# Giving a quarter of a long convolution's transposes to the DMA engines, with ScalarE and VectorE work re-ordered around it

## The chip, the core and the metric

The kernel runs on one core of a Trainium2 chip. The metric is the device time of one execution in microseconds (us), from the hardware; lower is better. The engines are named as in the profile: PE is TensorE (with PEld, its weight loads), ACT is ScalarE, DVE is VectorE, POOL is GpSimd, SP is SyncE, whose queue (SPq) issues nearly all DMAs here.

## What is computed

There are 64 batches (NB), 128 channels (H) and 2048 time steps (T). First each batch's channels are mixed by one of 16 weight matrices, with a residual. Then each channel is convolved over time with its own long kernel K, masked behind a length, and added.

```python
x = x + einsum('bct,bcd->bdt', x, weights[condition])          # step 1
K = 2 * real(einsum('hn,hnl->hl', Ct, exp(dtA[:, :, None] * arange(2048))))   # per channel, 64 modes
y = irfft(rfft(x, 4096) * rfft(K, 4096))[..., :2048] + x * D[:, None]         # step 2: causal convolution
x = x + y * (arange(2048) < length[:, None])
```

## The kernel before

**Two stages.** In the first some 325 us the mixing matmuls run (`L529`), batch by batch, and their results u go to a scratch tensor in HBM, laid out by channel; beside them VectorE works out tables for K. The rest, some 750 us, is the convolution, done as a state-space scan in blocks: time is cut into 8 blocks of Q = 256, and the work goes by **pairs of channels**, 64 pairs (`PAIRS`), one after the other. The change is in this second stage alone.

**One pair.** `u_row` holds a pair's two channels as rows: 128 partitions (64 batches by 2 halves of time) by 4 groups `g` of 256 values, in f32. The matmuls want time on the partitions, so PE transposes each 128x128 piece into a PSUM bank (`transpose_u`, `L541`): 16 a pair, four (g = 0 to 3) into each of banks 4 to 7; the bank is called q = 0 to 3 (channel q // 2, half-block q % 2). ACT copies a bank as the f16 high part into `u_t` (`u_hi`, step "u" of ACT, `L722`), and DVE writes the f16 remainder beside it (`u_lo`, step "u" of DVE, `L986`). Then

- `inputs_to_state` (`L555`, 12 matmuls) adds up what each block puts into the state. It needs all four quarters of `u_t`, and `gt_sb`, which is made by two DMA transposes of `g_sb` (`L317`);
- `advance` for j = 1 to 6 (`L567`, 6 matmuls each) carries the state from block to block. Each needs the state before it: ACT copies its high part out of PSUM (`state_hi`, "s", `L730`), DVE its low part (`state_lo`, "s", `L991`), and only then may PE go on. I call the states s1 to s7;
- `out_part` for k = 0 to 7 (`L590`, `L596`, `L599`) makes the outputs from `u_t`, from the taps `toep`, and from the states. ACT takes them out of PSUM (`out_evac`, "o", `L738`), DVE lays the unmasked values over them (`overlay`, "o", `L1016`), SP stores them.

**Two helpers of `out_part`.** `toep` holds zeros in part of its lower 64 partitions; `fold_toeplitz` ("t", `L1008`) copies taps there. `first_half` ("x", `L1001`, two copies a pair, of f16 64x2048) builds `x_t` out of `u_t`.

**Slots.** Every engine has the same outer loop: slot c does, interleaved in an order written out by hand (`steps` in each engine's `slot`), the states of pair c, the outputs of pair c - 1, and the transposes of pair c + 1. On PE, slot c is out_part(0), out_part(1), `inputs_to_state(c)`, then out_part(k) and advance(k - 1) for k = 2 to 7; two transposes are put into each out_part, `between(2k)` and `between(2k + 1)`. Engines work through their lists strictly in order, with semaphores between them. So a step of DVE that is late makes all the steps behind it in the list late.

**GpSimd** makes the factors for later pairs, without waiting for the slot: `g_lo` (`L424`, after ACT's `g_hi`, step "g", `L674`), then at once the products of the pair after that: twice g_x (`L415`), twice g_y (`L415`), and g_x minus g_y (`L419`).

**SP's order in a slot:** load half of `u_row`, the two transposes of `g_sb`, two stores, load the other half of `u_row`, load `toep`, two stores (which wait for DVE's overlay).

Of the kernel before, what the change touches and what calls it, by code (L numbers as in the profile page):

```python
# [40 lines left out]
WAVES = 5  # L41
XS = 6
# [24 lines left out]
def build(nc, x, cond, length, w_in, log_dt, c_in, log_a, a_im, d_in, out):  # L67
# [6 lines left out]
    with ctx:  # L74
# [16 lines left out]
        eyes = sb("eyes", [P, 2, NM], F16)  # L91
        swap = sb("swap", [P, 2, NM], F16)
# [103 lines left out]
        s_st, s_sth, s_stl = (sem(n) for n in ("s_st", "s_sth", "s_stl"))  # L196
        s_xt, s_tz = sem("s_xt"), sem("s_tz")
# [56 lines left out]
        def _(sp):  # L254
# [65 lines left out]

            def store_out(i, c, h):
# [25 lines left out]
            def slot(i, c):  # L347
# [129 lines left out]
        def _(pe):  # L477
# [55 lines left out]
            def transpose_u(i, c, k):  # L533

                q, g, n = k // NG, k % NG, UN * i + c
                if k % 8 == 0:
# [6 lines left out]
                if g == NG - 1:  # L543
# [105 lines left out]
        def _(act):  # L649
# [94 lines left out]
            first = (("u", 0, 3), ("g", 2, 0), ("s", 0, 1), ("s", 0, 2), ("s", 0, 3), ("u", 1, 0), ("s", 0, 4),  # L744
                     ("s", 0, 5), ("u", 1, 1), ("s", 0, 6), ("u", 1, 2))

            def slot(i, c):
                steps = (("s", c - 1, 7), ("u", c, 3), ("o", c - 2, 3), ("g", c + 2, 0), ("u", c + 1, 0),
                         ("o", c - 1, 0), ("s", c, 1), ("s", c, 2), ("u", c + 1, 1), ("s", c, 3),
                         ("o", c - 1, 1), ("s", c, 4), ("s", c, 5), ("u", c + 1, 2),  # L750
                         ("s", c, 6), ("o", c - 1, 2))
                for what, of, k in steps if c else first:
# [20 lines left out]
        def _(dve):  # L773
# [295 lines left out]
```

## Time and profile before

| | |
|---|---|
| three runs, median (lowest to highest) | 1081.11 us (1080.15 to 1083.68) |
| profiled execution | 1082.12 us, of which its span is 1080.3 us |
| granted TensorE clock, mean | 0.996 |
| PE, DVE, ACT, POOL busy | 93%, 71%, 51%, 47% of the span |
| mean of one `u_hi` (ACT, 512 columns) and one `state_hi` (128 columns) | 595 and 276 ns |
| mean of one `u_lo` (DVE, 512 columns) and one `state_lo` (128 columns) | 689 and 290 ns |

The busy times are of one profiled execution. A matmul's busy time overlaps that of the next, so PE's work is better read from the starts of its rows in the timeline. Rows of the timeline carry the start, the duration, the engine and the line; what stands in brackets is how long the engine sat idle just before, and what released it. A row's duration on DVE and POOL takes in time that the instruction spends issued but held up.

### The profile page before, as it was taken

The page shows a single profiled execution, that of the slowest core. Times are in us where ns is not written, and L with a number is a line of the kernel's source. Part 1 is how long each engine was busy: PE and PEld are TensorE (multiplying, and loading weights), DVE is VectorE, ACT ScalarE, POOL GpSimd, SP SyncE. Part 2 cuts the span into 40 slices and gives each one's busy share as a digit, 9 for nine tenths or more (in the row PEclk, how much of TensorE's full clock was granted, in tenths as well). Part 3 has the DMA queues.
Part 4 walks back from the last instruction along what each step waited for, and adds up shares of the span by engine and source line. Part 5 has one row for each costly group of instructions (what it writes and reads, how often), then busy time and mean ns, then how long its engine had stood idle before and what let it go on. Part 6 is the DMA issues. An engine that isn't in the chain of part 4 may idle for free.

```text
span 1080.3 us, 29253 instructions
## 1 busy us (share of the span) xinstructions
PE 1004.6 (93%) x11632; PEld 739.8 (68%) x11632; DVE 772.3 (71%) x1711; ACT 548.5 (51%) x1166; POOL 502.7 (47%) x545
## 2 busy tenths in 40 slices
PE   8977788777899999999999999999999999999998
PEld 5322234233347888888888788888888888888886
DVE  4989940000017888888888888888888888888885
ACT  2634334244444556556456555555555555555553
POOL 2200042101205556656666665665665665665530
PEclk9999999999999999999999999999999999999999
DMA  8999999999989999999999999999999999999994
GB/s 343 423 423 423 424 422 422 377 424 424 423 326 294 284 271 262 228 227 224 217 239 233 214 238 224 225 234 228 222 232 226 234 221 229 225 225 232 208 223 118
DMA packets 169543, 304.96 MB, mean 282 GB/s; under 512 B 78194, under 2 KB 111346, under 8 KB 161218
## 3 DMA queue, kind: packets, MB, share of 16 engines
q1 hardware_dynamic: 169090, 302.64, 98.4%
q8 instruction: 94, 1.54, 0.6%
q14 instruction: 39, 0.32, 0.1%
q10 hardware_dynamic: 160, 0.26, 0.1%
q0 software_dynamic: 160, 0.20, 0.1%
HBM read 152.37 MB, written 134.41 MB: 265 GB/s over the span
## 4 chain that ended last, share of the span: by engine, by line
PE 74%; DMA 18%; ACT 3%; DVE 2%; issue 2%; SPq 1%; ACTq 0%
DMA u_scratch<-stage 17%; PE bank L590 16%; PE bank L599 15%; PE bank L555 13%; PE bank L541 10%; PE bank L529 7%; PE bank L567 7%; PE bank L596 5%; ACT stage L708 2%; DVE x_t L1001 1%; PE bank L608 1%; DMA x_f<-in_x 1%; DVE st_sb L991 0%; ACT ring L708 0%; DVE u_t L986 0%
## 5 line engine op out<-in xcount | busy, mean ns | idle before, releaser
L590 PE MATMUL bank<-toep,u_t 128*128 128x192 f16 (+1 forms) x3072 | 342.7, 220 | 2.0 <-issue 1.8
L599 PE MATMUL bank<-g_sb,st_sb 128*128 128x256 f16 x1536 | 305.9, 273 | 0.5 <-issue 0.4
L529 PE MATMUL bank<-x_f,w_buf 128*128 128x512 f32 x512 | 237.3, 608 | 57.2 <-ACT stage L708 35.5
L541 PE MATMUL bank<-ident,u_row 128*128 128x128 f32 x1024 | 277.4, 274 | 0.2
L730 ACT ACTIVATE st_sb<-bank 128x128 f16<-128x128 f32 x448 | 123.8, 276 | 289.6 <-PE bank L567 198.0
L590 PEld LDWEIGHTS bank<-toep,u_t 128*128 128x128 f16 x3072 | 231.3, 98 | 16.3 <-issue 2.4
L529 PEld LDWEIGHTS bank<-x_f,w_buf 128*128 128x128 f32 x512 | 93.4, 192 | 192.4 <-issue 109.8
L1016 DVE COPY_PREDICATED o_sb<-mask,u_row 128x512 f32<-128x512 uint8 x256 | 205.8, 804 | 16.6 <-issue 16.5
L986 DVE SCALAR_TENSOR_TENSOR u_t<-bank,u_t 128x512 f16<-128x512 f32 x256 | 176.2, 689 | 37.4 <-ACT u_t L722 35.4
L596 PE MATMUL bank<-toep,x_t 128*128 128x64 f16 x2048 | 188.3, 193 | 1.9 <-issue 1.9
L431 POOL TENSOR_TENSOR lam_sb<-eyes,lam_v 128x512 f16<-128x512 f16 x64 | 75.2, 1176 | 235.7 <-PE bank L567 235.7
L722 ACT ACTIVATE u_t<-bank 128x512 f16<-128x512 f32 x256 | 152.2, 595 | 54.4 <-PE bank L541 50.7
L708 ACT ACTIVATE stage<-bank 128x1024 f32<-128x1024 f32 x100 | 96.8, 1021 | 148.7 <-DMA u_scratch<-stage 124.1
L991 DVE TENSOR_TENSOR st_sb<-bank,st_sb 128x128 f16<-128x128 f32 x448 | 129.7, 290 | 56.2 <-ACT st_sb L730 52.6
L596 PEld LDWEIGHTS bank<-toep,x_t 128*128 128x128 f16 x2048 | 157.5, 98 | 2.1 <-issue 2.1
L555 PE MATMUL bank<-u_t,gt_sb 128*128 128x448 f16 x768 | 155.7, 352 | 1.3 <-DVE u_t L986 1.3
L738 ACT ACTIVATE o_sb<-bank 128x512 f32<-128x512 f32 x256 | 153.2, 599 | 4.1 <-PE bank L599 4.0
L599 PEld LDWEIGHTS bank<-g_sb,st_sb 128*128 128x128 f16 x1536 | 149.3, 98 | 5.8
L541 PEld LDWEIGHTS bank<-ident,u_row 128*128 128x128 f32 x1024 | 143.8, 141 | 9.7 <-issue 1.5
L567 PE MATMUL bank<-st_sb,lam_sb 128*128 128x64 f16 x2304 | 130.0, 193 | 4.8 <-DVE st_sb L991 3.4
L439 POOL TENSOR_TENSOR w_buf<-w_f,ident 128x128 f32<-128x128 f32 x64 | 33.5, 527 | 210.3 <-PE bank L529 205.1
L567 PEld LDWEIGHTS bank<-st_sb,lam_sb 128*128 128x128 f16 x2304 | 107.4, 97 | 32.9 <-issue 10.0
(135 smaller groups left out, 912.6 us busy)
## 6 DMA issues: line engine op xcount, KB each, us to landing
x_f<-in_x SPq DMA_DIRECT2D x64, 1024.0 KB, 19.6
u_row<-u_scratch SPq DMA_DIRECT2D x128, 512.0 KB, 5.7
out<-o_sb SPq DMA_DIRECT2D x254, 256.0 KB, 3.8
u_scratch<-stage SPq DMA_DIRECT2D x50, 1024.0 KB, 17.8
toep<-k_scratch SPq DMA_DIRECT2D x64, 256.0 KB, 6.0
u_scratch<-ring SPq DMA_DIRECT2D x13, 512.0 KB, 14.7
u_scratch<-kept SPq DMA_DIRECT2D x10, 448.0 KB, 7.0
gt_sb<-g_sb SPq DMA_TRANSPOSE x124, 5.4
```

What stands on the lines that cost most here:

```text
L529: last = pe.matmul(bank[:, 4 * (n % 2) + k, :], w_buf[n % XS][:, :], x_f[n % XS][:, k * 512:(k + 1) * 512], start=True, stop=True)
L541: last = pe.transpose(bank[:, 4 + q, g * P:(g + 1) * P], u_row[c % 4][:, h, g, tb * P:(tb + 1) * P], ident[:, :])
L555: last = pe.matmul(bank[:, h, 0:(NJ - 1) * NB], gt_sb[c % 2][:, h, a, 1 - tb, :], u_t[c % 4][:, h, tb, b, 0:(NJ - 1) * NB], start=(m == 0) ...
L567: last = pe.matmul(bank[:, h, at(j):at(j) + NB], lam_sb[c % 2][:, h, a, :, :].rearrange("p k m -> p (k m)"), st_sb[c % 2][:, h, b, at(j):a ...
L590: pe.matmul(bank[:, y, col + tb * P + NM:col + Q], u[:, h, tb, a, rows_], t[:, h, b, NM:Q - tb * P], start=first, stop=False, skip_group_c ...
L596: pe.matmul(bank[:, y, col + tb * P:col + tb * P + NM], x_t[c % 2][:, h, tb, rows_], t[:, h, b, 0:NM], start=False, stop=False, skip_group ...
L599: last = pe.matmul(bank[:, y, col:col + Q], st[:, h, a, gr * ROWS:(gr + 1) * ROWS], g[:, h, b, :], start=False, stop=(m == 2), skip_group_ ...
L722: act.activation(u_t[c % 4][:, q // 2, q % 2, 0, :], bank[:, 4 + q, :], ACT.Copy, scale=US)\
L738: act.activation(o_sb[o][:, 2 * (v % 2):2 * (v % 2) + 2, :].rearrange("p g t -> p (g t)"), bank[:, 2 + v % 2, :], ACT.Copy, scale=1.0 / (U ...
L986: dve.scalar_tensor_tensor(out=t[:, q // 2, q % 2, 1, :], in0=bank[:, 4 + q, :], scalar=US, in1=t[:, q // 2, q % 2, 0, :], op0=MUL, op1=SU ...
L991: dve.tensor_tensor(out=state(st_sb[c % 2], 1, j), in0=new_state(j), in1=state(st_sb[c % 2], 0, j), op=SUB).then_inc(s_stl, 1)
L1016: dve.copy_predicated(o_sb[2 * (c % 2) + v // 2][:, g2, :].rearrange("p g (b t) -> p (g b) t", t=P), mask[:, g2, :].rearrange("p g (b t) - ...
```

## The change

**The last group of both channels.** From pair 3 on (`TURNED`), PE leaves out g = 3 in all four banks (`groups` gives 3 and not 4, for both channels, `TH = 2`). So four of a pair's 16 transposes go, and `u_hi` and `u_lo` handle 384 columns and not 512. In their place ACT makes the f16 high part of that group straight from `u_row` (`parts_hi`, step "p"), DVE the low part (`parts_lo`, "p"), into a new tile `parts`; and SP issues one DMA transpose, 128x1024 in f16, from `parts` into `u_t` (`transpose_parts`), between the load of `toep` and the stores that follow it.

**The fold** of the taps ("t") goes from DVE to ACT.

**The order on DVE.** "x" twice and the new "p" now stand ahead of the slot's first state, and "u" and the first "o" of the slot behind states 1 and 2.

```diff
+        parts = sb("parts", [P, TH, 2, 2, P], F16)
+        def groups(c, h):
+            return NG - 1 if c >= TURNED and h < TH else NG
...
+            def transpose_parts(c):
+                sp.wait_ge(s_pl, c - TURNED + 1)
+                wait(sp, s_out, 4 * (c - 3))
+                sp.dma_start(ap(u_t[c % 4], (NG - 1) * ROWS, [[NG * ROWS, TH * 4], [1, ROWS]]),
+                             parts[:, :, :, :, :].rearrange("p h b a t -> p (h b a t)"), transpose=True)\
+                    .then_inc(s_pt, 16)
...
+                if TURNED <= c + 1 < PAIRS:
+                    transpose_parts(c + 1)
                 if has(i, c - 1):
                     store_out(i, c - 1, 0)
...
+                if g >= groups(c, q // 2):
+                    return
...
                 pe.wait_ge(s_ul, 4 * n + 4)
+                wait(pe, s_pt, 16 * (n - TURNED + 1))
...
+            def parts_hi(c):
+                for h in range(TH):
+                    act.wait_ge(s_row[c % 4][h], 16 * (c // 4 + 1))
+                wait(act, s_pt, 16 * (c - TURNED))
+                act.activation(parts[:, :, :, 0, :],
+                               u_row[c % 4][:, 0:TH, NG - 1, :].rearrange("p h (b t) -> p h b t", t=P),
+                               ACT.Copy, scale=US).then_inc(s_ph, 1)
...
                 steps = (("s", c - 1, 7), ("u", c, 3), ("o", c - 2, 3), ("g", c + 2, 0), ("u", c + 1, 0),
-                         ("o", c - 1, 0), ("s", c, 1), ("s", c, 2), ("u", c + 1, 1), ("s", c, 3),
+                         ("o", c - 1, 0), ("p", c + 1, 0), ("t", c, 0), ("s", c, 1), ("s", c, 2), ("u", c + 1, 1), ("s", c, 3),
...
+            def parts_lo(c):
+                dve.wait_ge(s_ph, c - TURNED + 1)
+                dve.scalar_tensor_tensor(out=parts[:, :, :, 1, :],
+                                         in0=u_row[c % 4][:, 0:TH, NG - 1, :].rearrange("p h (b t) -> p h b t", t=P),
+                                         scalar=US, in1=parts[:, :, :, 0, :], op0=MUL, op1=SUB).then_inc(s_pl, 1)
...
                 if part == 0:
                     dve.wait_ge(s_ul, 4 * n + 4)
+                    wait(dve, s_pt, 16 * (n - TURNED + 1))
...
-                steps = (("s", c - 1, 7), ("u", c, 3), ("o", c - 2, 3), ("t", c, 0), ("u", c + 1, 0),
-                         ("o", c - 1, 0), ("s", c, 1), ("x", c, 0), ("s", c, 2), ("x", c, 1), ("s", c, 3),
+                steps = (("s", c - 1, 7), ("u", c, 3), ("o", c - 2, 3), ("x", c, 0), ("x", c, 1), ("p", c + 1, 0),
+                         ("s", c, 1), ("u", c + 1, 0), ("s", c, 2), ("o", c - 1, 0), ("s", c, 3),
                          ("u", c + 1, 1), ("s", c, 4), ("o", c - 1, 1), ("s", c, 5), ("u", c + 1, 2), ("s", c, 6), ("o", c - 1, 2))
```

On DVE, in a slot of the steady stage, this stood in the program before, from `u_lo` of the pair's last quarter (`L986`) to the third state (`L991`):

```order
L986 SCALAR_TENSOR_TENSOR u_t<-bank,u_t 128x512
L1014 MEMSET pad 1x1
L1016 COPY_PREDICATED o_sb<-mask,u_row 128x512
L1008 COPY toep<-toep 64x4x64
L986 SCALAR_TENSOR_TENSOR u_t<-bank,u_t 128x512
L1014 MEMSET pad 1x1
L1016 COPY_PREDICATED o_sb<-mask,u_row 128x512
L991 TENSOR_TENSOR st_sb<-bank,st_sb 128x2x64
L1001 COPY x_t<-u_t 64x2048
L991 TENSOR_TENSOR st_sb<-bank,st_sb 128x2x64
L1001 COPY x_t<-u_t 64x2048
L991 TENSOR_TENSOR st_sb<-bank,st_sb 128x2x64
```

After the change the same piece reads as follows (`L1031` is "u", `L1061` "o", `L1053` "x", `L1036` the new "p", `L1042` the states):

```order
L1031 SCALAR_TENSOR_TENSOR u_t<-bank,u_t 128x384
L1059 MEMSET pad 1x1
L1061 COPY_PREDICATED o_sb<-mask,u_row 128x512
L1053 COPY x_t<-u_t 64x2048 x2
L1036 SCALAR_TENSOR_TENSOR parts<-u_row,parts 128x4x128
L1042 TENSOR_TENSOR st_sb<-bank,st_sb 128x2x64
L1031 SCALAR_TENSOR_TENSOR u_t<-bank,u_t 128x384
L1042 TENSOR_TENSOR st_sb<-bank,st_sb 128x2x64
L1059 MEMSET pad 1x1
L1061 COPY_PREDICATED o_sb<-mask,u_row 128x512
L1042 TENSOR_TENSOR st_sb<-bank,st_sb 128x2x64
```

Between "o" of pair c - 2 and the first state there now stand x, x and p, where t, u and o stood; u and the first o of pair c - 1 have moved behind the first and the second state.

On ACT, in the same slot, the piece from `g_hi` to the second state was this before, and is this now (`L752` is `parts_hi`, `L760` the fold):

```order
L674 ACTIVATE g_sb<-g_x 128x2x256
L722 ACTIVATE u_t<-bank 128x512
L738 ACTIVATE o_sb<-bank 128x512
L730 ACTIVATE st_sb<-bank 128x2x64 x2
L722 ACTIVATE u_t<-bank 128x512
```

```order
L695 ACTIVATE g_sb<-g_x 128x2x256
L744 ACTIVATE u_t<-bank 128x384
L777 ACTIVATE o_sb<-bank 128x512
L752 ACTIVATE parts<-u_row 128x4x128
L760 ACTIVATE toep<-toep 64x4x64
L769 ACTIVATE st_sb<-bank 128x2x64 x2
```

Two instructions have come in ahead of the first state, behind the output's copy. GpSimd's program is the same as before.

## Rows read from the trace of the kernel before

**Rows 1.** One line's instructions, the fold `L1008`, from 400 to 1000 us
```profile
engine op xcount: duration ns min/median/max, first and last start us, forms
L1008 DVE COPY toep<-toep x51: 1026/1031/1040, 408.2 to 989.9; 64x256 f16<-64x256 f16 x51
```

**Rows 2.** Timeline of PE in one slot: start us, duration us, engine, line
```profile
803.15 2.43 PE L555 MATMUL bank<-u_t,gt_sb 128*128 128x448 f16 x12
...
806.09 0.27 PE L541 MATMUL bank<-ident,u_row 128*128 128x128 f32 x1
806.20 0.38 PE L599 MATMUL bank<-g_sb,st_sb 128*128 128x256 f16 x2
806.43 0.34 PE L567 MATMUL bank<-st_sb,lam_sb 128*128 128x64 f16 x6
```

**Rows 3.** Timeline rows of all engines in another slot, 1003 to 1009 us
```profile
1003.40 1.66 POOL L415 TENSOR_TENSOR g_y<-alpha_im,beta_im 128x256 f32<-128x256 f32 x2
1003.63 0.98 DVE L1016 COPY_PREDICATED o_sb<-mask,u_row 128x512 f32<-128x512 uint8 x1
...
1005.13 1.27 POOL L419 TENSOR_TENSOR g_x<-g_x,g_y 128x512 f32<-128x512 f32 x1
1005.50 1.45 DVE L1001 COPY x_t<-u_t 64x2048 f16<-64x2048 f16 x1
...
1006.99 0.29 DVE L991 TENSOR_TENSOR st_sb<-bank,st_sb 128x128 f16<-128x128 f32 x1
1007.31 0.69 DVE L1001 COPY x_t<-u_t 64x2048 f16<-64x2048 f16 x1
1007.42 0.33 PE L567 MATMUL bank<-st_sb,lam_sb 128*128 128x64 f16 x6 [0.42 <-DVE st_sb L991]
1007.80 0.28 ACT L730 ACTIVATE st_sb<-bank 128x128 f16<-128x128 f32 x1 [0.38 <-PE bank L567]
...
1008.11 0.29 DVE L991 TENSOR_TENSOR st_sb<-bank,st_sb 128x128 f16<-128x128 f32 x1
...
1008.59 0.34 PE L567 MATMUL bank<-st_sb,lam_sb 128*128 128x64 f16 x6
```

**Rows 4.** Timeline rows of all engines in slot 0, 325 to 328 us
```profile
325.20 1.65 POOL L415 TENSOR_TENSOR g_x<-alpha_re,beta_re 128x256 f32<-128x256 f32 x2
...
325.35 2.04 DVE L1001 COPY x_t<-u_t 64x2048 f16<-64x2048 f16 x2
...
327.42 0.29 DVE L991 TENSOR_TENSOR st_sb<-bank,st_sb 128x128 f16<-128x128 f32 x1
...
327.86 0.31 PE L567 MATMUL bank<-st_sb,lam_sb 128*128 128x64 f16 x5 [0.63 <-DVE st_sb L991]
```

**Rows 5.** Timeline of DVE in the slot of rows 2
```profile
802.64 0.74 DVE L1016 COPY_PREDICATED o_sb<-mask,u_row 128x512 f32<-128x512 uint8 x1
...
803.41 1.03 DVE L1008 COPY toep<-toep 64x256 f16<-64x256 f16 x1
...
805.09 1.03 DVE L1016 COPY_PREDICATED o_sb<-mask,u_row 128x512 f32<-128x512 uint8 x1
...
806.02 0.27 DVE L991 TENSOR_TENSOR st_sb<-bank,st_sb 128x128 f16<-128x128 f32 x1
...
808.38 0.29 DVE L991 TENSOR_TENSOR st_sb<-bank,st_sb 128x128 f16<-128x128 f32 x1 [0.23 <-ACT st_sb L730]
```

**Rows 6.** Timeline of POOL and of ACT in the same slot
```profile
803.07 1.29 POOL L424 TENSOR_TENSOR g_sb<-g_x,g_sb 128x512 f16<-128x512 f32 x1 [0.61 <-ACT g_sb L674]
804.32 1.19 POOL L415 TENSOR_TENSOR g_x<-alpha_re,beta_re 128x256 f32<-128x256 f32 x2
...
802.35 0.64 ACT L674 ACTIVATE g_sb<-g_x 128x512 f16<-128x512 f32 x1
```

**Rows 7.** SP's queue: its waits from 400 to 1000 us (total us, times, longest), and a timeline row
```profile
SPq L330 <- DVE o_sb L1016: 153.5, 53, 4.1
...
801.70 2.55 SPq L317 DMA_TRANSPOSE gt_sb<-g_sb  x2
```

**Rows 8.** DMA issues on the page: count, median us from issue to landing
```profile
gt_sb<-g_sb SPq DMA_TRANSPOSE x124, 5.4
```

More of the change, by code:

```diff
@@ L41 @@
 WAVES = 5
+TURNED = 3
+TH = 2
 XS = 6
@@ L196, in build @@
         s_st, s_sth, s_stl = (sem(n) for n in ("s_st", "s_sth", "s_stl"))
+        s_ph, s_pl, s_pt = (sem(n) for n in ("s_ph", "s_pl", "s_pt"))
         s_xt, s_tz = sem("s_xt"), sem("s_tz")
@@ L721, in u_hi, with fold_toeplitz @@
                     wait(act, s_out, 4 * (n - 3))
-                act.activation(u_t[c % 4][:, q // 2, q % 2, 0, :], bank[:, 4 + q, :], ACT.Copy, scale=US)\
+                cols = groups(c, q // 2) * ROWS
+                act.activation(u_t[c % 4][:, q // 2, q % 2, 0, 0:cols], bank[:, 4 + q, 0:cols], ACT.Copy, scale=US)\
                     .then_inc(s_uh, 1)
+            def parts_hi(c):
[5 more added lines that the diff above has]
+                               ACT.Copy, scale=US).then_inc(s_ph, 1)
+            def fold_toeplitz(i, c):
+                act.wait_ge(s_t[c % 4], 16 * (i + c // 4 + 1))
+                act.activation(toep[c % 4][0:NM, :, :, 0:NM].rearrange("p h a t -> p (h a) t"),
+                               toep[c % 4][NM:P, :, :, 0:NM].rearrange("p h a t -> p (h a) t"), ACT.Copy)\
+                    .then_inc(s_tz, 1)
             def state_hi(i, c, j):
@@ L742, in _ @@
                 u_hi(0, 0, q)
-            first = (("u", 0, 3), ("g", 2, 0), ("s", 0, 1), ("s", 0, 2), ("s", 0, 3), ("u", 1, 0), ("s", 0, 4),
+            first = (("u", 0, 3), ("t", 0, 0), ("g", 2, 0), ("s", 0, 1), ("s", 0, 2), ("s", 0, 3), ("u", 1, 0), ("s", 0, 4),
                      ("s", 0, 5), ("u", 1, 1), ("s", 0, 6), ("u", 1, 2))
@@ L762, in slot @@
                             u_hi(i, of, k)
+                        elif what == "p":
+                            if of >= TURNED:
+                                parts_hi(of)
                         elif what == "o":
                             out_evac(i, of, k)
+                        elif what == "t":
+                            fold_toeplitz(i, of)
                         else:
@@ L985, in u_lo @@
                 t = u_t[c % 4]
-                dve.scalar_tensor_tensor(out=t[:, q // 2, q % 2, 1, :], in0=bank[:, 4 + q, :], scalar=US,
-                                         in1=t[:, q // 2, q % 2, 0, :], op0=MUL, op1=SUB).then_inc(s_ul, 1)
+                cols = groups(c, q // 2) * ROWS
+                dve.scalar_tensor_tensor(out=t[:, q // 2, q % 2, 1, 0:cols], in0=bank[:, 4 + q, 0:cols], scalar=US,
+                                         in1=t[:, q // 2, q % 2, 0, 0:cols], op0=MUL, op1=SUB).then_inc(s_ul, 1)
+            def parts_lo(c):
[3 more added lines that the diff above has]
+                                         scalar=US, in1=parts[:, :, :, 0, :], op0=MUL, op1=SUB).then_inc(s_pl, 1)
             def state_lo(i, c, j):
@@ L1034, in slot @@
                             state_lo(i, of, k)
-                        elif what == "t":
-                            fold_toeplitz(i, of)
                         elif what == "u":
                             u_lo(i, of, k)
+                        elif what == "p":
+                            if of >= TURNED:
+                                parts_lo(of)
                         elif what == "x":
```

8 lines of the change are left out of this document (2 added, 6 removed).

## The prediction

> **What bounds the kernel now.** I first took the page's busy shares (93% PE), then PE's timeline of a steady slot, because matmul busy times overlap and starts don't. PE runs there without a gap worth the name: from `L555` to the first `advance` is 3.28 us (803.15 to 806.43), and a transpose takes 0.11 us of it (806.09 to 806.20, whatever its own 0.27 says) [rows 2]. Behind PE stands a second bound that the shares don't show: the chain of states. Where PE had to wait for it, the trace gives its bare length: `advance` starts at 1007.42, ACT's state 0.38 later and for 0.28, DVE's at 1008.11, which is 0.03 after that, for 0.29; and from the end of such a DVE row (1006.99 + 0.29 = 1007.28) to PE's start is 0.14. That is 0.38 + 0.28 + 0.03 + 0.29 + 0.14 = 1.12 us. A step of PE (out_part and `advance`) is 1.17 (1007.42 to 1008.59) [rows 3]. So the chain hides behind PE with 0.05 us to spare, and a state that DVE takes late is paid by PE in full.
>
> **What makes DVE late.** A fold of 64x256 takes 1.03 us, 51 times alike [rows 1], though a copy of 64x2048 takes 0.69 [rows 3]. It is issued at 803.41 and ends at 804.44, just behind POOL's `L424`, which ran from 803.07 to 804.36 [rows 5, 6]. The same shows with "x": issued at 1005.50 while POOL's `L419` ran until 1006.40, it ended at 1006.95, took 1.45, made the state behind it late, and PE idled 0.42 us [rows 3]. And "o" at 805.09 ended at 806.12, 0.61 behind POOL's g_x pair (804.32 + 1.19 = 805.51) [rows 5, 6]. I read: a DVE "x", "t" or "o" and a POOL instruction exclude each other, and the later one waits for the whole of the earlier. "u" and "s" read PSUM, and in the slot of rows 5 none of them is stretched. Who wins where both have a queue? Slot 0 is the natural experiment. There two "x" stand back to back beside POOL's two g_x: 2.04 us for the two, 1.02 each and not 0.69, and the g_x pair takes 1.65 and not 1.19. They alternate. The state behind them came at 327.42, and PE idled 0.63 us [rows 4, 6]. The Trainium skill, page "SBUF — State Buffer", section "SBUF: two separate sides", states such a rule: VectorE instructions in a two-port mode or with two SBUF inputs and GpSimd's hold a shared pair of ports as an exclusive lock, for the whole instruction. The trace agrees (1.45 and 1.03 us above). By that rule the new "p" too, with two SBUF inputs, would queue for it.
>
> **The change, part by part.** All times are in the slot of rows 2, 5 and 6, with what came before `L555` kept in place.
>
> *Four transposes go.* They are the second of the two in out_part(1), (3), (5) and (7). That of out_part(1) lies outside the chain: 0.11 us saved; `L555` starts at 803.04. Those of the other three would make steps of 1.06, below the chain's 1.12: each saves only 0.05. Together 0.26 us a slot, over 61 slots 16 us; with no chain it would be 4 x 0.11 x 61 = 27 us.
>
> *`u_hi` and `u_lo` are a quarter shorter.* From the table, (595 - 276)/384 x 128 = 0.11 us on ACT and (689 - 290)/384 x 128 = 0.13 on DVE. So the first "o" of the slot ends not at 803.38 but 0.24 earlier, at 803.14. ACT's `g_hi` ends 0.11 earlier (802.99 to 802.88), and POOL's `L424` is issued at 802.96 [rows 5, 6].
>
> *ACT gets "p" and "t".* Its nearest rows are `g_hi`, 0.64, for "p" (same shape and kinds) and a state copy of 128 columns, 0.28, to a `u_hi` of 0.6 (table) for "t" [rows 3, 6]. Some 1.0 to 1.2 us; `L555` alone runs 2.4 us there [rows 2] and ACT has only one "u" and one "o" (1.2) in it. I take them as hidden. If that cover were gone, the first state would be late by what is over.
>
> *DVE gets x, x, p ahead of the first state.* Here is the price. `L424` has ended 0.98 behind the end of the "o" before it (803.38 to 804.36); so now at 803.14 + 0.98 = 804.12. The first x, issued at 803.17, is behind `L424` in the queue for the ports, and ends 0.55 behind it (as 1006.40 to 1006.95): 804.67. POOL's first g_x has been waiting, and takes its turn; the second x ends 1.02 later: 805.69. The second g_x ends 1.02 - 0.55 = 0.47 behind that, 806.16; p, with 512 columns and two inputs in SBUF like "o", ends 0.6 behind it: 806.76. The state may start 0.10 before the end of such a row (806.12 to 806.02): 806.66. `advance` follows the start of s1 by 0.41 (806.02 to 806.43): 807.07. From `L555` that is 4.03 us where 3.28 stood: **+0.75 us** a slot. Bounds for p: if it asks for no shared port, it ends at 805.75 + 0.69 = 806.4 and the term is +0.4; if x and p never had to wait, they end at 805.3, and the term is nothing.
>
> *What is late next.* The first "o" of pair c - 1 now stands behind s2. s2 starts 1.12 after s1, at 807.78, and "o" some 0.2 later, at 807.99. POOL, freed when p ends: its first g_y 0.45 later (in rows 3 the g_y pair ends at 1005.06, 0.45 behind the "o" that ended at 1004.61), the second 0.6 later, then `L419` after 0.07 (1005.06 to 1005.13): it asks at 806.76 + 1.12 = 807.88. It is ahead of "o" by 0.11 us. Then "o" waits for its 1.27 us, until 809.15, and ends at 809.15 + 0.61 = 809.76; s3 starts at 809.66. From s1 to s3 is then 3.00 us; before it was 2.36 (806.02 to 808.38) [rows 5]: **+0.64**.
>
> *SP gets one transpose more.* In a slot SP waits 153.5/53 = 2.9 us for DVE's overlay, at just the place where the new one is put in, and the two of `g_sb`, together as many bytes, take it 2.55 us [rows 7]. It fits, and in a longer slot all the more. To landing those take 5.4 us [rows 8]; the new one is wanted a good 7 us after its issue.
>
> **The sum.** With both terms: 0.75 + 0.64 - 0.11 - 2 x 0.05 = +1.18 us a slot. This holds in the slots with a "p" and a full POOL, 2 to 61, which is 60: +71 us. Some of today's stalls (the 0.42 above) are of the same making and don't come on top; I take off 6, a choice. Against the profiled execution's own 1082.1 us (1 us above the median of the runs) that is about 1147; on the median's scale **1146 us**.
>
> **The rivals.**
> 1. *As above* (slower, 1146; 1132 to 1160). It hangs on an order won by 0.11 us. Chance 0.42.
> 2. *"o" gets in ahead of `L419`.* Then only the first term stands: 0.75 - 0.11 - 3 x 0.05 = +0.49, 60 times, less the same 6: +23, or 1104 us (1090 to 1118). For it speaks that 0.11 us is of the size of my rounding, against it that a fold issued 0.34 behind `L424` had to wait [rows 5, 6]. Chance 0.27.
> 3. *The ports don't bind in the new order* (faster): the waits of DVE stay below 0.1 us a slot because POOL's instructions fall elsewhere. Then PE's 0.26 us stands, in 61 slots: 16 us, 1065 (1054 to 1076). It decides from s1 starting before 805.9. For it speaks that DVE has 0.9 us less to do a slot (fold 1.03 and 4 x 0.13 go, p 0.69 comes). Against it stands slot 0. Chance 0.17.
> 4. *It comes out even*, with a first term of about 0.3 us: 1078 to 1084. Chance 0.08.
> 5. *The new transpose lands late.* It stands behind the load of `toep` in the queue, and DVE's first x waits for it with all that is behind x. If it landed 1 us late each slot, PE's gain would turn into 60 x (1 - 0.26) = +44 us, 1125. Against it: 5.4 against 7 us. Chance 0.06.
>
> **How the numbers follow.** A measurement here tells about 0.3% from no change (3 us). Faster is case 3, 0.17; same is case 4, 0.08; slower are cases 1, 2 and 5, 0.75. The time is case 1's. The range, 1080 to 1160 us, takes in cases 1, 2, 5 and most of 4, and leaves out case 3 and what lies above p's bound, 2 in 10 together.
>
> **What would show it.** On the after-profile: the two x with over 0.9 us each where their pair lies beside the g_x pair, which is itself stretched beyond 1.19; s1 of DVE about 3.6 us behind `L555`'s start where it is 2.87 now; idle time of PE's `advance` put down to DVE's state, some 40 us over the stage or more, against 0.4 here and there; the first "o" behind s2 at 1.7 us or more (case 1) or at 0.74 (case 2). Four transposes fewer a pair, 244 in all, in PE's count. I am wrong if the x pair takes 1.4 us, if s1 is on time, or if the idle time before `advance` or `L555` is put down to the DMA.

## The result, and the profile after

The changed kernel takes **1151.8 us** (median of 4, 1150.5 to 1153.4). The kernel before took 1082.4 beside it on the same chip (4 runs, 1080.2 to 1084.5). The ratio is 1.064, with a 95% interval of 1.061 to 1.067: slower. The prediction was 1146 us, slower. Two of the four executions of one kernel below (f4) were over 1.5% above its fastest, and its ratio is of the other two alone.

The page of the changed kernel's profile (busy us and share of the span; then groups: busy, mean ns | idle before):

```profile
PE 1006.2 (88%) x11388; PEld 705.7 (61%) x11388; DVE 824.8 (72%) x1708; ACT 585.3 (51%) x1291; POOL 503.4 (44%) x545
...
L561 PE MATMUL bank<-ident,u_row 128*128 128x128 f32 x780 | 210.8, 275 | 0.0
...
L588 PE MATMUL bank<-st_sb,lam_sb 128*128 128x64 f16 x2304 | 129.5, 192 | 64.7 <-DVE st_sb L1042 63.8
...
L1053 DVE COPY x_t<-u_t 64x2048 f16<-64x2048 f16 x128 | 161.6, 1262 | 12.1 <-issue 8.2
L576 PE MATMUL bank<-u_t,gt_sb 128*128 128x448 f16 x768 | 157.4, 355 | 7.8 <-DMA u_t<-parts 6.5
```

PE is down from 93% to 88% and has 780 transposes, 244 fewer than its 1024. Nothing of that shows in the time: its `advance` (`L588`) sat idle 64.7 us, nearly all of it for DVE's low part of a state. A 64x2048 copy "x" now takes 1262 ns on average (median 998, against 707 before).

One slot in order of time, the rows of DVE, POOL, ACT's states, and PE where the chain goes through it (start us, duration us, engine, line; in brackets the idle time before and its releaser). It answers to the slot of [rows 2, 5, 6]:

```profile
836.59 2.43 PE L576 MATMUL bank<-u_t,gt_sb 128*128 128x448 f16 x12
836.65 1.16 POOL L442 TENSOR_TENSOR g_sb<-g_x,g_sb 128x512 f16<-128x512 f32 x1 [0.60 <-ACT g_sb L695]
836.74 2.65 DVE L1053 COPY x_t<-u_t 64x2048 f16<-64x2048 f16 x2
...
837.76 2.10 POOL L433 TENSOR_TENSOR g_x<-alpha_re,beta_re 128x256 f32<-128x256 f32 x2
...
839.05 0.28 ACT L769 ACTIVATE st_sb<-bank 128x128 f16<-128x128 f32 x1 [0.66 <-PE bank L576]
...
839.42 1.00 DVE L1036 SCALAR_TENSOR_TENSOR parts<-u_row,parts 128x512 f16<-128x512 f32 x1
...
839.83 1.64 POOL L433 TENSOR_TENSOR g_y<-alpha_im,beta_im 128x256 f32<-128x256 f32 x2
840.34 0.28 DVE L1042 TENSOR_TENSOR st_sb<-bank,st_sb 128x128 f16<-128x128 f32 x1
...
840.76 0.34 PE L588 MATMUL bank<-st_sb,lam_sb 128*128 128x64 f16 x6 [0.75 <-DVE st_sb L1042]
...
841.14 0.28 ACT L769 ACTIVATE st_sb<-bank 128x128 f16<-128x128 f32 x1 [1.80 <-PE bank L588]
...
841.45 0.29 DVE L1042 TENSOR_TENSOR st_sb<-bank,st_sb 128x128 f16<-128x128 f32 x1 [0.36 <-ACT st_sb L769]
...
841.55 1.27 POOL L437 TENSOR_TENSOR g_x<-g_x,g_y 128x512 f32<-128x512 f32 x1
841.66 1.75 DVE L1061 COPY_PREDICATED o_sb<-mask,u_row 128x512 f32<-128x512 uint8 x1
...
842.30 0.28 ACT L769 ACTIVATE st_sb<-bank 128x128 f16<-128x128 f32 x1 [0.48 <-PE bank L588]
...
843.31 0.27 DVE L1042 TENSOR_TENSOR st_sb<-bank,st_sb 128x128 f16<-128x128 f32 x1
...
844.10 0.28 ACT L769 ACTIVATE st_sb<-bank 128x128 f16<-128x128 f32 x1 [1.02 <-PE bank L588]
```

Read it from ACT's first state at 839.05. DVE's half of that state would follow at once; it comes at 840.34, because x, x and p stand ahead of it and go turn by turn with POOL: the x pair takes 2.65 us, the g_x pair 2.10, p 1.00. So the second state of ACT comes 2.09 us behind the first (841.14 - 839.05). Then POOL's difference (`L437`) starts at 841.55 and "o" at 841.66, 0.11 us too late: it takes 1.75, DVE's third state starts at 843.31, and ACT's fourth comes 1.80 behind the third (844.10 - 842.30). All other distances in this slot are 1.12 to 1.17.

These distances between ACT's states are a good ruler, because any lateness of any engine in the chain shows in them. The table below gives, for each kernel that was run, the mean distance from the first state of a slot to that of the next, from 450 to 1100 us of its trace (some 50 slots), and the two distances that matter, as they repeat from slot to slot (medians or near them; a slot's mean takes in the longer slots too). It is worked out from the timeline rows of ACT's state copies.

```
                            transfer  first->second  third->fourth  slot, mean   median of runs
before                         no         1.22           1.11         11.65        1082
after                          yes        2.08           1.84         12.74        1151.8
order only (e1)                no         1.20           1.12         11.57        1081.9
moved back (e2)                yes        1.69           1.18         12.28        1122.8
short difference (e3)          yes        2.08           1.17         12.29        1126.1
short gpsimd (e4)              yes        1.2 to 1.5     1.17         11.92        1104.7
no transfer (e7)               no         2.08           1.84         12.74        1145.7
transfer alone (e8)            yes        1.21           1.12         11.94        1101.0
short gpsimd, no transfer (e9) no         1.47           1.17         11.46        1072.7
parts alone (e10)              no         2.08           1.70         12.96        1158.3
short difference, no tr. (f1)  no         2.08           1.17         12.05        1106.8
short products, no tr. (f2)    no         1.46           1.17         11.47        1074.3
moved back, no transfer (f3)   no         1.68           1.18         11.72        1088.5
parts a pair ahead (f4)        yes        1.18           1.17         13.71        1209.7
```

"Transfer" means that one DMA transposition of 128x1024 halves runs in each slot besides the two of `g_sb`. It brings some 1000 more packets of 256 bytes a slot (94,729 of them in e8's trace from 450 to 1000 us, 48,128 in e1's).

### The profile page after: what moved, and what is told of

It is laid out like the page before. It is cut to its first block, busy times and chain, and to the rows that moved or that the text cites. A ratio compares the mean times of both kernels' runs of the same rounds, so it can differ in the third digit from the quotient of the medians.

```text
span 1148.8 us, 29130 instructions
## 1 busy us (share of the span) xinstructions
PE 1006.2 (88%) x11388; PEld 705.7 (61%) x11388; DVE 824.8 (72%) x1708; ACT 585.3 (51%) x1291; POOL 503.4 (44%) x545
## 4 chain that ended last, share of the span: by engine, by line
PE 34%; DVE 23%; DMA 18%; issue 15%; ACT 7%; SPq 2%; ACTq 0%
DMA u_scratch<-stage 16%; DVE x_t L1053 12%; PE bank L588 7%; PE bank L547 7%; PE bank L611 6%; PE bank L620 6%; DVE parts L1036 5%; DVE st_sb L1042 4%; PE bank L561 3%; DVE u_t L1031 3%; ACT u_t L744 2%; PE bank L617 2%; PE bank L576 2%; DMA u_t<-parts 2%; ACT stage L729 2%
## 5 line engine op out<-in xcount | busy, mean ns | idle before, releaser
L620 PE MATMUL bank<-g_sb,st_sb 128*128 128x256 f16 x1536 | 279.5, 273 | 0.2 <-issue 0.2
L1061 DVE COPY_PREDICATED o_sb<-mask,u_row 128x512 f32<-128x512 uint8 x256 | 246.7, 964 | 16.3 <-issue 16.3
L561 PE MATMUL bank<-ident,u_row 128*128 128x128 f32 x780 | 210.8, 275 | 0.0
L449 POOL TENSOR_TENSOR lam_sb<-eyes,lam_v 128x512 f16<-128x512 f16 x64 | 78.3, 1223 | 301.2 <-PE bank L588 301.2
L588 PE MATMUL bank<-st_sb,lam_sb 128*128 128x64 f16 x2304 | 129.5, 192 | 64.7 <-DVE st_sb L1042 63.8
L1042 DVE TENSOR_TENSOR st_sb<-bank,st_sb 128x128 f16<-128x128 f32 x448 | 128.6, 287 | 80.1 <-ACT st_sb L769 80.0
L588 PEld LDWEIGHTS bank<-st_sb,lam_sb 128*128 128x128 f16 x2304 | 98.0, 97 | 125.2 <-issue 95.4
L1053 DVE COPY x_t<-u_t 64x2048 f16<-64x2048 f16 x128 | 161.6, 1262 | 12.1 <-issue 8.2
L576 PE MATMUL bank<-u_t,gt_sb 128*128 128x448 f16 x768 | 157.4, 355 | 7.8 <-DMA u_t<-parts 6.5
L1031 DVE SCALAR_TENSOR_TENSOR u_t<-bank,u_t 128x384 f16<-128x384 f32 (+1 forms) x256 | 142.4, 557 | 20.7 <-ACT u_t L744 9.9
L620 PEld LDWEIGHTS bank<-g_sb,st_sb 128*128 128x128 f16 x1536 | 132.6, 98 | 7.3 <-issue 1.4
L744 ACT ACTIVATE u_t<-bank 128x384 f16<-128x384 f32 (+1 forms) x256 | 125.1, 489 | 10.6 <-PE bank L561 10.2
L433 POOL TENSOR_TENSOR g_x<-alpha_re,beta_re 128x256 f32<-128x256 f32 x128 | 129.6, 1031 | 0.2 <-POOL st_sb L468 0.2
```

What stands on the lines that cost most here:

```text
L561: last = pe.transpose(bank[:, 4 + q, g * P:(g + 1) * P], u_row[c % 4][:, h, g, tb * P:(tb + 1) * P], ident[:, :])
L576: last = pe.matmul(bank[:, h, 0:(NJ - 1) * NB], gt_sb[c % 2][:, h, a, 1 - tb, :], u_t[c % 4][:, h, tb, b, 0:(NJ - 1) * NB], start=(m == 0) ...
L588: last = pe.matmul(bank[:, h, at(j):at(j) + NB], lam_sb[c % 2][:, h, a, :, :].rearrange("p k m -> p (k m)"), st_sb[c % 2][:, h, b, at(j):a ...
L620: last = pe.matmul(bank[:, y, col:col + Q], st[:, h, a, gr * ROWS:(gr + 1) * ROWS], g[:, h, b, :], start=False, stop=(m == 2), skip_group_ ...
L1031: dve.scalar_tensor_tensor(out=t[:, q // 2, q % 2, 1, 0:cols], in0=bank[:, 4 + q, 0:cols], scalar=US, in1=t[:, q // 2, q % 2, 0, 0:cols], ...
L1042: dve.tensor_tensor(out=state(st_sb[c % 2], 1, j), in0=new_state(j), in1=state(st_sb[c % 2], 0, j), op=SUB).then_inc(s_stl, 1)
```

## The experiments

Each ratio is against executions of the kernel before that were taken beside the run; their medians lie between 1079.9 and 1082.4 us. So a difference of two medians below can be off by 2 us.

**e1, the new order alone.** No parts, no transposition; ACT keeps the fold, DVE the new order.

```diff
-TURNED = 3
+TURNED = 64
```

> The changed kernel with no pair's group turned by the DMA engines: all 16 transposes back on PE, no p steps, but the fold on ScalarE and VectorE's new order (x and x ahead of the first state, o behind the second). Port theory (VectorE's x, o, p and GpSimd's instructions take turns): without p the second x ends about 1.0 us earlier, the first state starts 2.8 to 2.9 us behind the first inputs_to_state matmul as before the change, and GpSimd has not reached its difference when o asks, so o takes under 1.1 us; 1075 to 1088 us. Rival, the order alone does it: some 1130 us or more.

Measured 1081.9 us (10 runs), ratio 0.9995 (0.998 to 1.001). In its timeline (DVE, POOL, ACT, PE):

```profile
826.21 2.43 PE L576 MATMUL bank<-u_t,gt_sb 128*128 128x448 f16 x12
...
826.52 2.54 DVE L1053 COPY x_t<-u_t 64x2048 f16<-64x2048 f16 x2
...
828.68 0.28 ACT L769 ACTIVATE st_sb<-bank 128x128 f16<-128x128 f32 x1 [0.96 <-PE bank L576]
...
829.09 0.29 DVE L1042 TENSOR_TENSOR st_sb<-bank,st_sb 128x128 f16<-128x128 f32 x1
...
830.59 0.74 DVE L1061 COPY_PREDICATED o_sb<-mask,u_row 128x512 f32<-128x512 uint8 x1
...
830.77 1.65 POOL L437 TENSOR_TENSOR g_x<-g_x,g_y 128x512 f32<-128x512 f32 x1
```

The x pair takes turns here as well, 2.54 us, and still the first state stands 2.88 us behind `L576`'s start, as it stood 2.87 behind `L555` before. The turns of the x pair fit ahead of the state. And "o" is now 0.18 us ahead of the difference: POOL waits, not DVE. So the order, and the fold on ACT, cost nothing by themselves. What p adds decides both.

**e2, DVE's old order,** with p in the fold's place.

```diff
-    ("o", c - 2, 3), ("x", c, 0), ("x", c, 1), ("p", c + 1, 0),
-    ("s", c, 1), ("u", c + 1, 0), ("s", c, 2), ("o", c - 1, 0), ("s", c, 3),
+    ("o", c - 2, 3), ("p", c + 1, 0), ("u", c + 1, 0),
+    ("o", c - 1, 0), ("s", c, 1), ("x", c, 0), ("s", c, 2), ("x", c, 1), ("s", c, 3),
```

> The changed kernel with VectorE's order of before, p in the place of the fold (s7, u, o, p, u, o, s1, x, s2, x, s3). Port theory: p waits for GpSimd's g_sb (1.5 us for p), then o waits for a product behind it; the first state starts 0.4 us late instead of 0.8, and no o meets GpSimd's difference; a slot of about 11.6 us, 1075 to 1092 us. Rival, the added DMA transposes and their waits cost the time: stays above 1130 us.

Measured 1122.8 us, ratio 1.036 (1.033 to 1.039): a miss by 31 us, that lies between the range and the rival's 1130. The first state is late by less, as expected (1.69 for 2.08), and no "o" meets the difference. Half its slots are 11.5 to 11.9 us, but the others take 12.0 to 15.5.

**e3, POOL's difference cut short,** 16 of 256 columns from the fifth pair on.

```diff
+    w = 16 if c >= 4 else Q
-    pool.tensor_tensor(out=g_x[r][:, :, :], in0=g_x[r][:, :, :], in1=g_y[r][:, :, :], op=SUB)
+    pool.tensor_tensor(out=g_x[r][:, :, 0:w], in0=g_x[r][:, :, 0:w], in1=g_y[r][:, :, 0:w], op=SUB)
```

> The changed kernel, but from pair 4 on GpSimd's difference g_x - g_y covers 16 of 256 columns (the taps of later pairs come out wrong, the sync is the same). Port theory: only the second term goes, o behind the second state takes under 1 us where it takes 1.75, the interval between the second and third state falls from 1.85 to about 1.2 us, the first state stays as late as it is; 1105 to 1122 us. Rival, that o is slow for another reason (ScalarE's copy, the mask): no change, 1150.

Measured 1126.1 us, ratio 1.040 (1.038 to 1.042), 4 above the range. The second lateness is gone (1.17 for 1.84), the first stays (2.08), but again every third slot or so is long.

**e4, all of POOL's products cut short too.** The same, and each product one row of 16.

```diff
+    m = 1 if c >= 4 else 16
-    out=ap(dst[r], h * Q, [[16, 16], [1, 16]]), in0=ap(ta, o, [[1, 16], [0, 16]]), in1=ap(tb, o, [[0, 16], [1, 16]])
+    out=ap(dst[r], h * Q, [[16, m], [1, 16]]), in0=ap(ta, o, [[1, m], [0, 16]]), in1=ap(tb, o, [[0, m], [1, 16]])
```

> As the run before, and GpSimd's four products too cover 16 of 256 columns from pair 4 on; its g_sb and lambda instructions keep their size. Port theory: x behind g_sb still waits, the second x and p take 0.6 to 0.8 us each, the first state is on time; what is left is PE's saving of 0.26 us a slot: 1060 to 1076 us. Chain theory of the transposes: if all four were worth their 0.11 us, 1055. Rival, DMA or SP bound: stays above 1090.

Measured 1104.7 us, ratio 1.021 (1.017 to 1.024): a miss by 29 us, on the side of the rival (DMA or SP bound, above 1090). Its short slots are 11.2 us, but with the long ones the mean is 11.92. Where POOL blocks next to nobody, something else makes slots long. Some waits of this kernel, from 450 to 1000 us (total us, times, longest):

```profile
PEld bank L590 <- issue: 13.9, 36, 1.3
DVE x_t L1055 <- issue: 9.5, 12, 2.1
...
PE bank L578 <- DMA u_t<-parts: 4.7, 5, 2.2
```

`L578` and x are the two readers of the transposed parts. `L578` waited for the transposition five times, up to 2.2 us; for x's twelve waits the profile names nothing. Three misses of one sign led to a second theory, B: the transfers cost time that a slot of 12.74 us hides. The next four kernels part transfers and engine work.

**e7, no transfer.** All of the engines' new work, but nothing carries the parts.

```diff
-TURNED = 3
+TURNED = 4
...
-    if TURNED <= c + 1 < PAIRS:
-        transpose_parts(c + 1)
...
-    wait(pe, s_pt, 16 * (n - TURNED + 1))
...
-    wait(dve, s_pt, 16 * (n - TURNED + 1))
...
-    wait(act, s_pt, 16 * (c - TURNED))
+    wait(act, s_pl, c - TURNED)
```

> The changed kernel without the new DMA transposition itself: ScalarE and VectorE still make the two parts of the last groups and TensorE still leaves four transposes out from the fourth pair on, but nothing carries the parts into the transposed tile (the last group's columns keep the values of an earlier pair, so the output differs there). Theory A (VectorE's x, x and low parts ahead of the first states, with GpSimd's products beside them, and the blend behind the second state make the 12.74 us slot; the transfer is hidden): 1140 to 1152 us. Theory B (the transfers are what makes it slower): 1125 us or less, down to 1070.

Measured 1145.7 us, ratio 1.060 (1.057 to 1.063). Its slots take 12.74 us like those of the changed kernel, with the same two late states. Theory A stands for the changed kernel: the engines make it slow. Some 5 of the 6 us between the two lie in the changed kernel's early slots, from 340 to 450 us, where the new transposition goes beside the last stores of the first stage: its first states are 4.9 us behind those of e7 at 457 us and 5.1 at 1107 us. One line's view of it there (issue time on SP; who waited; time to landing), and below it the same view after 450 us:

```profile
L333 SPq DMA_TRANSPOSE u_t<-parts x8: 1302/2386/4082, 354.5 to 446.7; - x8
...
  PE bank L576: 6.5, 5
...
DMA to landing us min/median/max: 5.7/6.9/8.7
```
```profile
L333 SPq DMA_TRANSPOSE u_t<-parts x51: 1256/1257/1928, 459.9 to 1097.1; - x51
...
DMA to landing us min/median/max: 5.2/5.8/7.3
```

**e8, the transfer alone:** e1 with a DMA transposition of `toep` into a tile that nobody reads; TensorE transposes all sixteen, and there is no p. (The load of `toep` waits for an earlier transposition too; that edit is left out here. No wait of an engine in its trace, from 450 to 1000 us, is put down to a DMA.)

```diff
-    sp.wait_ge(s_pl, c - TURNED + 1)
-    wait(sp, s_out, 4 * (c - 3))
-    sp.dma_start(ap(u_t[c % 4], (NG - 1) * ROWS, [[NG * ROWS, TH * 4], [1, ROWS]]),
-                 parts[:, :, :, :, :].rearrange("p h b a t -> p (h b a t)"), transpose=True)
+    sp.wait_ge(s_tz, c)
+    sp.wait_ge(s_xt, 2 * c)
+    wait(sp, s_pt, 16 * (c - TURNED))
+    sp.dma_start(turned[:, :, :],
+                 toep[(c - 1) % 4][:, :, :, :].rearrange("p h a t -> p (h a t)"), transpose=True)
```

> The kernel with VectorE's and ScalarE's new order alone (it took 1081.9 us) plus one DMA transposition of 128 x 1024 halves a slot, of a tap tile into a tile that nobody reads; TensorE transposes all sixteen and no parts are made. Theory A (transfers are hidden): 1078 to 1086 us. Theory B (the added transfers delay the other transfers, above all the transposed g): 1095 to 1120 us.

Measured 1101.0 us, ratio 1.018 (1.014 to 1.021). Nobody waits for this transfer, and it costs 19 us against e1. Where? In PE's waits "for issue", that is for nothing that the profile shows. First e8, then e1, from 450 to 1000 us:

```profile
PEld bank L589 <- issue: 9.0, 15, 1.8
PEld bank L612 <- issue: 4.7, 5, 1.5
PEld bank L618 <- issue: 3.8, 5, 1.1
...
PEld bank L563 <- issue: 2.5, 4, 1.4
...
PEld bank L621 <- issue: 1.6, 1, 1.6
PEld bank L577 <- issue: 1.4, 2, 0.9
```
```profile
PEld bank L611 <- issue: 2.7, 4, 1.5
...
PEld bank L588 <- issue: 0.7, 3, 0.3
```

That is 23.0 us against 3.9 (two rows of 0.3 and 0.2 are not shown for e1). Most of it is a few waits of about a microsecond, ahead of any line at all. Three of them in e8's timeline:

```profile
721.69 0.11 PEld L612 LDWEIGHTS bank<-toep,u_t 128*128 128x128 f16 x2 [1.15 <-issue]
...
756.41 0.10 PEld L618 LDWEIGHTS bank<-toep,x_t 128*128 128x128 f16 x1 [1.10 <-issue]
...
791.08 0.11 PEld L589 LDWEIGHTS bank<-st_sb,lam_sb 128*128 128x128 f16 x2 [0.92 <-issue]
```

These three stand 34.7 us apart, each ahead of another line. A wait tied to the data would stand ahead of one line. I read them as PE waiting for its own code, which comes by DMA as well. The profile has a queue for it (packets, MB, share of the 16 engines; e8, from 450 to 1000 us), in packets of 16 KB:

```profile
q8 instruction: 63, 1.03, 0.8%
```

The trace bears this out. Packets of that queue end at 720.19, 754.95 and 789.55 us, and PE goes on 1.50, 1.46 and 1.53 us after them. Of the 19 gaps of 0.5 us or more in PE's weight loads from 450 to 1000 us, 16 end 1.2 to 1.6 us behind the end of such a packet; with a packet each 8.7 us, about one of them would do so by chance. These 16 add up to 17.0 us; e1 has one, of 1.5. And the gaps go by PE's program, not by time: counted in the trace's records of its weight loads and waits, most of e8's stand 400 or 533 apart, and e2, e3 and e4, whose PE programs are the same, all have one at the 3571st record (518.37, 515.80 and 507.83 us) and at the 9448th (923.14, 921.60 and 901.87 us). Why a packet comes late beside the transfer is not shown: one lasts about as long in e8 as in e1 (medians 0.97 and 0.96 us), and no kernel here changes the code's arrival alone.

**e9, short POOL work without the transfer:** the edits of e4 and of e7 together.

> The kernel with GpSimd's products and difference cut short from the fifth pair on (1104.7 us), now without the new transposition as well (the last group's columns keep old values; the kernel's output leaves out both). Its short slots took 11.17 us, every third or so 12.5 to 15.4. Theory B2 (the long slots come from the transfers): all slots near 11.2, so 1060 to 1070 us. Rival (they come from elsewhere, as from the engines' order): 1095 to 1107 us.

Measured 1072.7 us, ratio 0.992 (0.990 to 0.995), 3 above the range. Without the transfer e4's long slots are gone (mean 11.46). They were the transfers', some 31 us by the ratios (1.021 against 0.992). PE's gaps behind a 16 KB packet add up to 21.3 us in e4, 17 of them from 450 to 1000 us, and there is none in e9; that is what the two slot means differ by in that time (0.46 us in some 47 slots).

**e10, the parts alone:** p on ACT and DVE as in the changed kernel, no transposition, and TensorE transposes all sixteen.

```diff
-    return NG - 1 if c >= TURNED and h < TH else NG
+    return NG
```

and the lines of e7 but for `TURNED`.

> ScalarE and VectorE make both parts of the last groups in the changed kernel's places, but nothing transposes them: TensorE transposes all sixteen, so this is the new order (1081.9 us) plus the two instructions for the parts. Theory A: the low parts push the first state late and the blend behind GpSimd's difference, as in the changed kernel: 1145 to 1165 us (at most sixteen us above the changed kernel, by the four transposes that TensorE does again). Theory B: the two instructions alone are worth at most what they last with nothing in turn, 0.4 us a slot, so 1082 to 1105 us.

Measured 1158.3 us, ratio 1.070 (1.067 to 1.073). Two instructions a slot are worth 76 us over e1 (1158.3 less 1081.9); DVE's p lasts 997 ns, as in the changed kernel. ACT's p is not what delays: in the changed kernel's slot above ACT was idle for 0.66 us ahead of its first state, waiting for PE. And against e7 it prices the four transposes, together with the quarter that `u_hi` and `u_lo` are shorter: 12.96 - 12.74 = 0.22 us a slot, 12.6 us in all. That is a net price, since the wait of "o" changes with it (1.70 for 1.84).

**f1 and f2: one term each.** Both are e7, f1 with the short difference of e3, f2 with the short products of e4 and the whole difference.

> The changed kernel without the transposition (1145.7 us), and from the fifth pair on GpSimd's difference takes 16 of 256 columns (the output leaves out both). Term 2 of the prediction (the first blend behind the second state waits for the difference, 0.64 us a slot) would be gone and term 1 (0.75) would stay: 1104 to 1114 us. Rival (the blend's wait only took up a lateness that the first state has anyway, or comes back elsewhere): 1125 us or more.

> The changed kernel without the transposition (1145.7 us), and from the fifth pair on GpSimd's four products are a sixteenth as long while its difference stays whole (the output leaves out both). VectorE's x, x and low parts then take turns with GpSimd's low part of g alone, so the first state is not late, and the difference is over before the blend comes. If both terms come from these turns: 1065 to 1082 us. Rival (x, x and the low parts are late by their own lengths): 1100 us or more.

f1: 1106.8 us, ratio 1.026 (1.024 to 1.029); f2: 1074.3 us, ratio 0.995 (0.993 to 0.997). Both as theory A had them: in f1 the second term goes and the first stays, in f2 nearly all of both goes. ACT's states in f1 and then in f2:

```profile
808.84 0.28 ACT L767 ACTIVATE st_sb<-bank 128x128 f16<-128x128 f32 x1 [0.67 <-PE bank L574]
810.92 0.28 ACT L767 ACTIVATE st_sb<-bank 128x128 f16<-128x128 f32 x1 [1.80 <-PE bank L586]
...
812.03 0.28 ACT L767 ACTIVATE st_sb<-bank 128x128 f16<-128x128 f32 x1 [0.43 <-PE bank L586]
...
813.21 0.28 ACT L767 ACTIVATE st_sb<-bank 128x128 f16<-128x128 f32 x1 [0.41 <-PE bank L586]
```
```profile
802.05 0.28 ACT L767 ACTIVATE st_sb<-bank 128x128 f16<-128x128 f32 x1 [0.66 <-PE bank L574]
803.52 0.28 ACT L767 ACTIVATE st_sb<-bank 128x128 f16<-128x128 f32 x1 [1.19 <-PE bank L586]
...
804.64 0.28 ACT L767 ACTIVATE st_sb<-bank 128x128 f16<-128x128 f32 x1 [0.44 <-PE bank L586]
```

In f1 the first distance is still 2.08, the third is 1.18: only the "o" was freed. In f2 the first falls to 1.47, and "o" is no longer late though the difference has its full length (1.17 in the table).

**f3: e2 without the transfer.**

> VectorE's old order with the low parts in the place of the fold (1122.8 us with the transposition), without the transposition (the last group's columns keep old values). Its ordinary slots took 11.56 to 11.72 us, others 12.2 to 15.4. If the long ones are late transfers: 1085 to 1098 us. Rival (they come from ScalarE's half of the parts, for which VectorE waits 1.3 to 2.6 us in each slot): 1110 us or more.

Measured 1088.5 us, ratio 1.010 (1.006 to 1.013). e2's long slots were the transfers' too, 34 us (32 against the kernels before beside them). DVE's wait for ACT's p, the rival here, is still there (60.7 us in 47 times from 450 to 1000 us), and the whole kernel is but 8.5 us above the kernel before.

**f4: the parts a pair ahead,** where POOL does nothing, and the transposition sent a slot before its reader.

```diff
 ACT: -  ("o", c - 1, 0), ("p", c + 1, 0), ("t", c, 0)
      +  ("o", c - 1, 0), ("t", c, 0)
      -  ("s", c, 4), ("s", c, 5), ("u", c + 1, 2)
      +  ("s", c, 4), ("s", c, 5), ("p", c + 2, 0), ("u", c + 1, 2)
 DVE: -  ("x", c, 0), ("x", c, 1), ("p", c + 1, 0)
      +  ("x", c, 0), ("x", c, 1)
      -  ("s", c, 6), ("o", c - 1, 2)
      +  ("s", c, 6), ("p", c + 2, 0), ("o", c - 1, 2)
 SP:  transpose_parts(c + 1) moved from behind load_toeplitz to behind transpose_g
```

> The changed kernel with the parts made one pair earlier: ScalarE's behind the fifth state, VectorE's behind the sixth, where GpSimd does nothing or makes the diagonal tile, and the transposition sent in the next slot behind those of g, a whole slot before its reader. If the low parts' place ahead of the first state is what costs: 1082 to 1105 us, of which up to 20 for the transfers' traffic and up to 16 back from TensorE's four transposes. Rival (the low parts cost about the same wherever they stand, VectorE being full): 1120 us or more. If the transfers' traffic is the second cost it should show as long slots still.

Measured 1209.7 us (median of 4, 1193 to 1218), ratio 1.110 (1.104 to 1.116): far above the range, and in the rival's (1120 or more), but not by the rival's mechanism, since both late states are gone (1.18 and 1.17 in the table). A wait from 450 to 1100 us, and one of them in its timeline:

```profile
ACT parts L752 <- DMA u_row<-u_scratch: 69.3, 28, 5.1
```
```profile
818.30 0.63 ACT L752 ACTIVATE parts<-u_row 128x512 f16<-128x512 f32 x1 [3.04 <-DMA u_row<-u_scratch]
...
853.88 0.28 ACT L769 ACTIVATE st_sb<-bank 128x128 f16<-128x128 f32 x1 [1.23 <-PE bank L576]
...
865.39 0.28 ACT L769 ACTIVATE st_sb<-bank 128x128 f16<-128x128 f32 x1 [1.23 <-PE bank L576]
```

I had looked at the engines and not at the data: the rows of pair c + 2 are still on their way, and ACT, waiting for them, holds its states back, in 28 of some 48 slots by 2.5 us each. A slot without this wait takes 11.51 us (865.39 - 853.88), like an ordinary one before the change (median 11.52), with p and the transfer in it. That speaks for a place where p is free, but does not show it: such slots mostly follow one of 15 us or more, in which the other engines could catch up. The loss is 119 us by the ratio, well above ACT's 69; the profile's mean granted clock is 0.951 too, 0.99 in the others. How the rest divides I did not settle. Loading `u_row` earlier wasn't tried.

No kernel with the transfer beats the kernel before.

## Why the prediction was right, and where it was off

**Term 1, x, x and p ahead of the first state (+0.75 us): right in its mechanism, 0.14 us short in size.** Counted from the start of PE's `inputs_to_state`, predicted and then measured in the slot above (start at 836.59): x pair over 2.65, 2.80; p over 3.72, 3.83; first state of DVE 3.62, 3.75; `advance` 4.03, 4.17, so that the term is 0.89 where 0.75 stood. e1, e10, e7 and f2 show the cause: the x pair with its turns fits, p does not, and with POOL's products short p takes 0.69 and not 1.00. Between f1 and f2 the turns are worth 0.58 us a slot; against a distance of 1.2 f2 keeps another 0.26, by which x, x and p are late even with POOL's products short. The Trainium skill, "SBUF — State Buffer", section "SBUF: two separate sides", has a VectorE instruction with two SBUF inputs and one of GpSimd that reads SBUF exclude each other for the whole instruction. The trace agrees: e7 and f2 differ in GpSimd's products alone, and p, with two SBUF inputs, takes 996 ns in e7 and 693 in f2.

**Term 2, "o" behind POOL's difference (+0.64): right,** and more exactly than the reading deserved. Predicted: the difference asks 0.11 us ahead of "o", and "o" takes 1.77; measured 0.11 (841.55, 841.66) and 1.75. e7 less f1 is 12.74 - 12.05 = 0.69 us a slot, 38.9 us. That "o" came second was won by no more than the 0.11 us that the prediction called the size of its rounding, so the choice between cases 1 and 2 has luck in it. Rival 2 was one order of two instructions away, and e1 shows it: there "o" is 0.18 ahead.

**The four transposes:** the sum took 0.11 + 2 x 0.05 = 0.21 us off for them (0.26 where the first term doesn't bind). e10 less e7 is 0.22, with the shorter copies in it: it fits, but doesn't price the transposes alone.

**The sum.** Predicted 1.18 us a slot over a slot without stalls, and 6 us off for today's; measured 12.74 - 11.52 = 1.22 over the median slot of before, and 12.74 - 11.65 = 1.09 over the mean, stalls and all. Times 60 the latter is 65, as forecast (71 less 6). The rest of the measured 69.4 us is what the transfer costs in this kernel, 5 to 6 us by e7, which the sum had put at nothing.

**Rival 5, the late landing:** 6.5 us of TensorE's idle time, in five early slots alone. I had taken one landing time (5.4 us) for all of the run [rows 8]; in the slots that still share the DMA engines with the first stage it was 6.9.

**Rival 3 was mis-sized, and so was its chance.** Its 1065 us, for ports that don't bind, took the DMAs as free. e9 has the ports (nearly) out of the way: 1072.7 us without the transfer, but e4, with it, 1104.7. Even nearly unhindered engines would have left this change slower than before. I had checked that the transposition *fits* (issue, landing), and not what its traffic does to everybody else. The chance of "faster", 0.17, rested on that.

The transfer has no single price. With minus without, each kernel first taken against the kernel before beside it, by the slot of the kernel without: 12.74 us: 5; 12.05: 17; 11.72: 32; 11.57 (e8 and e1): 20; 11.46: 31. It is least in the longest slot, but the rest doesn't go in order of room; in e8 nobody waits for the transfer, in the others two readers do. TensorE's gaps behind a 16 KB packet, from 450 to 1000 us, with and without the transfer, are 3.4 and 0.8 us (changed kernel, e7), 18.5 and 0.9 (e3, f1), 17.1 and 0 (e2, f3), 17.0 and 1.5 (e8, e1), 21.3 and 0 (e4, e9). So most of the price that the prediction had at nothing is TensorE waiting for its code. That the long slot of the changed kernel hides it because TensorE waits for DVE there anyway is my reading and not shown.

## What to carry to other kernels

When DVE and GpSimd work side by side, write out the turns: who asks for the shared ports when, and which instruction of the critical chain stands behind the loser. Here that gave the four times compared above to within 0.15 us. A DVE instruction that lasts 0.7 us when nothing holds it up cost 1.4 us a slot (e10 less e1, with ACT's half beside it), because it pushed two others over an edge.

A transfer moved off TensorE must be priced twice: for its readers, and for what shares the DMA engines with it, the engines' own code too. Test it with a copy of the transfer that nobody reads.

Don't take a hidden cost for no cost. In the changed kernel the transfer seemed worth 6 us; in the four other pairs of kernels it was 17 to 32.

## What the hardware showed beside the question

A DMA transposition of 128x1024 halves a slot, which nobody waits for, made TensorE's weight loads idle by 23.0 instead of 3.9 us in 550, mostly in pieces of about 1 us with no releaser in the profile. They end 1.2 to 1.6 us behind a 16 KB packet of the instruction queue, and kernels with the same TensorE program have them at the same places of it. I had not expected a price on TensorE itself.

Two back-to-back "x" beside POOL's pairs take 2.54 us (e1) and 2.65 us (changed kernel) for the two; one that nothing holds up lasts 0.69 [rows 3]. And a whole POOL difference takes 1.27 us when it comes ahead of "o" but 1.65 when it comes behind it: the loser's waiting is in its own duration, so here a stretched row names the victim, and the row of the other engine that ends inside it the culprit.
